# Moving part of a state sum from GpSimd and VectorE to ScalarE and accumulating DMAs, in a macaron block with a selective scan

## What is computed

```
x = x + 0.5 * ffn(layernorm(x))
x = x + ssm(layernorm(x))
x = x + 0.5 * ffn(layernorm(x))
```

```
def step(s, inp):
    u_t, d_t, B_t, C_t = inp
    dA = exp(d_t[..., None] * A)
    dBu = d_t[..., None] * B_t[:, None, :] * u_t[..., None]
    s = dA * s + dBu
    y = einsum('bin,bn->bi', s, C_t)
    return (s, y)
```

## Time and profile before

| | us |
|---|---|
| median of 3 runs | 2955.68 |
| lowest and highest of them | 2943.15, 2956.81 |
| the profiled execution | 2946.41 |
| its span | 2944.6 |
| PE busy | 2434.3 (83% of the span) |
| DVE busy | 2496.5 (85%) |
| POOL busy | 2260.7 (77%) |
| ACT busy | 1754.9 (60%) |

### The profile page before, as it was taken

The page is one execution under the profiler, slowest core; times in us unless marked ns, Lnnn a source line. Parts: engine busy times, 40 slices in busy tenths (PEclk is TensorE's granted clock), DMA queues, the critical chain, the costliest instruction groups (busy, mean ns, idle before and its releaser), DMA issues. The chain is left out here.

```text
span 2944.6 us, 38165 instructions
## 1 busy us (share of the span) xinstructions
PE 2434.3 (83%) x12266; PEld 1988.3 (68%) x12266; DVE 2496.5 (85%) x3131; ACT 1754.9 (60%) x2995; POOL 2260.7 (77%) x1370
## 2 busy tenths in 40 slices
PE   6677778788877898879978899888988796589968
PEld 5566667567666776667756787667776685478757
DVE  5549898788998998899977898899987898899973
ACT  5446567576656666655755557576666566565532
POOL 2238868887986889869996689978798688979852
PEclk9768989888989999989988799898998897699979
DMA  7634562673578367855687356874567555756634
GB/s 272 234 121 146 180 238 98 211 246 130 193 257 297 115 202 242 315 192 161 198 281 270 124 176 215 289 287 135 177 234 284 205 188 206 253 180 203 214 133 141
DMA packets 293951, 606.65 MB, mean 206 GB/s; under 512 B 23024, under 2 KB 23792, under 8 KB 293744
## 3 DMA queue, kind: packets, MB, share of 16 engines
q1 hardware_dynamic: 293744, 604.13, 59.8%
HBM read 451.47 MB, written 152.57 MB: 205 GB/s over the span
## 5 line engine op out<-in xcount | busy, mean ns | idle before, releaser
L1886 POOL TENSOR_TENSOR sbuf<-dus,bring 128x1024 f32<-128x1024 f32 x512 | 1221.9, 2402 | 252.0 <-PE pt L1363 134.1
L1513 ACT ACTIVATE pa<-dls,cst 128x512 f32<-128x512 f32 x1024 | 691.0, 688 | 456.9 <-DVE sbuf L1687 438.1
L1363 PE MATMUL pt<-ident,sbuf 128*128 128x128 f32 x4096 | 663.0, 300 | 244.7 <-DVE sbuf L1687 114.7
L1363 PEld LDWEIGHTS pt<-ident,sbuf 128*128 128x128 f32 x4096 | 527.9, 154 | 389.1 <-DVE sbuf L1687 155.6
L1283 PE MATMUL pm<-xT,wring 128*128 128x512 f32 x2816 | 711.7, 401 | 18.3 <-ACT spx L1427 8.8
L1687 DVE TENSOR_TENSOR_SCAN sbuf<-pa,carry,sbuf 128x512 f32<-128x512 f32 x512 | 635.3, 1267 | 67.5 <-POOL sbuf L1886 44.7
L1687 DVE TENSOR_TENSOR_SCAN sbuf<-pa,sbuf 128x512 f32<-128x512 f32 x512 | 608.7, 1210 | 64.7 <-ACT pa L1513 60.4
L1295 PE MATMUL pm<-wring,act 128*128 128x512 f32 x2176 | 585.9, 413 | 50.8 <-DVE hd L1615 22.6
L1283 PEld LDWEIGHTS pm<-xT,wring 128*128 128x128 f32 x2816 | 518.7, 190 | 121.8 <-issue 20.6
L1698 DVE SCALAR_TENSOR_TENSOR acc<-pt,cT,acc 128x512 f32<-128x512 f32 x768 | 547.6, 737 | 61.3 <-PE pt L1363 57.7
L1295 PEld LDWEIGHTS pm<-wring,act 128*128 128x128 f32 x2176 | 406.2, 195 | 143.9 <-issue 27.3
(11 more groups left out here) (137 smaller groups left out, 2274.6 us busy)
## 6 DMA issues: line engine op xcount, KB each, us to landing
wring<-wsp SPq DMA_DIRECT2D x408, 512.0 KB, 4.3
bring<-b_d SPq DMA_DIRECT2D x256, 256.0 KB, 3.8
xn_d<-tb SPq DMA_DIRECT2D x24, 1024.0 KB, 9.7
xnb<-xn_d SPq DMA_DIRECT2D x19, 1024.0 KB, 7.3
x_d<-tb SPq DMA_DIRECT2D x16, 1024.0 KB, 5.8
u_d<-hd SPq DMA_DIRECT2D x64, 256.0 KB, 4.1
sg_d<-hd SPq DMA_DIRECT2D x64, 256.0 KB, 3.9
tb<-x_d SPq DMA_DIRECT2D x16, 1024.0 KB, 7.3
```

The lines of the kernel that those rows point to most:

```text
L1363: ins = e.matmul(pt[u.pt[tt]][:, k * P:(k + 1) * P], sbuf[:, u.s3, k, tt * P:(tt + 1) * P], ident[:, :], is_transpose=True, start=True, st ...
L1513: e.activation(pa[k % 2][:, :], dls[:, k, :], ACT.Exp, scale=col(C_A + (4 * u.ig + k) * N + u.n)).then_inc(S.a_exp, 1)
L1886: e.tensor_tensor(sbuf[:, u.s3, h * m:(h + 1) * m, :], dus[:, h * m:(h + 1) * m, :], bring[:, u.s2:u.s2 + 1, :].broadcast_to([P, m, TC]), ...
```

## The change

The 15 groups before the last one sum their states in another way. The last group stays as it was.

- States 0, 3, 5, 8, 10 and 13 (`MOVED`): ACT scales all four quarters into `tmp`, which now has four tiles, [128, 4, 512]. No add follows on an engine. The whole tmp goes to y_d by one DMA: for state 0 a plain store, issued by SP; for the other five an accumulating DMA issued by POOL, which adds tmp to what lies in y_d.
- The ten other states are summed in acc by DVE. The first of them, n = 1, writes acc by a multiply alone; it takes the place of ACT's write.
- After state 15 acc is added to y_d by an accumulating DMA issued by POOL; the plain store from SP is gone.
- Each of these seven DMAs waits until the one before it has landed (the semaphores st_t, ac_t, ac_y), and the next moved state can be written to tmp when the DMA from tmp has landed. State 1 of the next group writes acc when the DMA from acc has landed.
- y_d is laid out by partition, so that each row of a DMA is 2048 contiguous elements of 4 bytes. The load of y (L2104 before) is of the same size.
- The planner counts a DMA on POOL with `ISSUE_POOL` = 1.0, and the order of all engines is planned anew. The kernel reserves 8192 as its `dynamic_dma_scratch_size`.

For one group the instructions change as follows:

| | before | after |
|---|---|---|
| ACT, scaled quarters | 16 | 24 |
| DVE, multiply and add | 48 | 36 |
| DVE, multiply alone | 0 | 4 |
| POOL, adds | 12 | 0 |
| POOL, accumulating DMAs of 1 MiB | 0 | 6 |
| SP, plain stores of 1 MiB | 1 | 1 |

```diff
-SHARED = (4, 8, 12)
+SHARED = (0, 4, 8, 12)
+MOVED = (0, 3, 5, 8, 10, 13)
...
             u.last = (c, u.ig) == (NCH - 1, 1)
+            u.moved = not u.last and u.n in MOVED
+            u.shared = u.last and u.n in SHARED
+            u.first = not u.last and u.n == 1
...
+            if u.moved:
+                u.y_before = sf("y_d")
+                u.t_kept = self.up(S.ac_t if u.n else S.st_t, 16)
+                self.sfree["tmp"] = self.sfree["y_d"] = (u.t_kept,)
...
-                u.y_kept = self.y_ready[c, u.ig] = self.up(S.st_y[u.ig], 16)
-                self.add("y_out", u)
+                u.y_before = sf("y_d")
+                u.y_kept = self.y_ready[c, u.ig] = self.up(S.ac_y[u.ig], 16)
...
-        tmp = sb("tmp", [P, TC])
+        tmp = sb("tmp", [P, 4, TC])
...
         def dve_states(units):
-                    if u.n == 0 or u.n in SHARED:
+                    if u.moved or u.shared:
...
+                        if u.first:
+                            e.tensor_scalar(a, x, scale, None, ALU.mult).then_inc(S.v_cmac, 1)
+                        else:
+                            e.scalar_tensor_tensor(a, x, scale, a, ALU.mult, ALU.add).then_inc(S.v_cmac, 1)
...
         def pool_states(units):
-                    if u.n not in SHARED:
-                        continue
-                    for tt in range(4):
-                        q.wait_ge(u.mul[tt], *u.acc_before[tt])
-                        e.tensor_tensor(acc[:, tt, :], acc[:, tt, :], tmp[:, :], ALU.add).then_inc(S.g_cadd, 1)
+                    if u.moved and u.n:
+                        q.wait_ge(u.mul[3], *u.y_before)
+                        e.dma_start(y_d[u.c, u.ig], tmp_row, accum_op=ALU.add).then_inc(S.ac_t, 16)
...
+                    elif u.n == N - 1 and not u.last:
+                        q.wait_ge(u.sum[3], *u.y_before)
+                        e.dma_start(y_d[u.c, u.ig], acc_row, accum_op=ALU.add).then_inc(S.ac_y[u.ig], 16)
...
-        def sp_y_out(units):
-                    q.wait_ge(u.sum[3])
-                    e.dma_start(rows(y_d[:, u.ig * 512:(u.ig + 1) * 512], u.c), acc[:, :, :]).then_inc(S.st_y[u.ig], 16)
+        def sp_t_out(units):
+                    q.wait_ge(u.mul[3], *u.y_before)
+                    e.dma_start(y_d[u.c, u.ig], tmp_row).then_inc(S.st_t, 16)
```

More of the change, by code:

```diff
@@ L65 @@
 DWELL = 12.0
-ISSUE, LAND = 0.42, 2.5
+ISSUE, ISSUE_POOL, LAND = 0.42, 1.0, 2.5
 LATE = {"pe": 0.3, "act": 0.13, "dve": 0.13, "pool": 0.15}
@@ L108, in begin @@
     def begin(self):
-        self.events, self.time, self.up, self.table = [], 0.0, None, None
+        self.events, self.time, self.up, self.table, self.moves = [], 0.0, None, None, False
     def wait_ge(self, *events):
@@ L168, in dma_start @@
         self.time += size / 370e3
+        self.moves = True
         return self
@@ L1229, in macaron @@
         y_rows = xT[:, :, :, :].bitcast(F32)
+        tmp_row = tmp[:, :, :].rearrange("p t n -> p (t n)")
+        acc_row = acc[:, :, :].rearrange("p t n -> p (t n)")
         small_m = NI * XW // 2
```

69 lines of the change are left out of this document (43 added, 26 removed).

## The result

| | us |
|---|---|
| before, median of 4 runs (lowest to highest) | 2950.48 (2943.15 to 2956.81) |
| after, median of 4 runs (lowest to highest) | 3004.65 (2998.87 to 3020.5) |
| ratio after / before, 95% interval | 1.0196 (1.0167 to 1.0224) |
| forecast, range | 2905, 2848 to 3015 |

The changed kernel is 2% slower. The forecast was 1.5% faster; the time lies in the range, and the direction was wrong.

A forecast was written before the change was run, and what follows sets the result against it. The prediction took DVE, POOL and PE to bound the kernel in turns, by stretches of 100 us. From 2946.4 us it took 77 of relief, added 30 for DMA overflow and 5 for landings: 2904, forecast as 2905, range 2848 to 3015.

The follow-up runs named there:

- e3: The changed kernel with y_d laid out by token, so accumulations go in rows of 2 KB instead of 8, same order; 3013.1 us, ratio 1.0232 to before.
- e1: The changed kernel, same order and issues, each of the 90 accumulations cut to 256 of 2048 columns (128 KB); 2878.6 us, ratio 0.9754 to before.

## What to carry to other kernels

Price a new DMA by what it does to the loads around it: how long it holds all engines in one piece, against how far ahead of their use the loads really land. A free mean share says nothing of that. An experiment that shrinks a transfer and leaves all instructions and their order in place parts relief from traffic in one run, and a second one with the same bytes in shorter pieces tells length from amount. And look for the free part of a change first: here more tiles of tmp gave 19 us in one plan, with no traffic at all, and nothing in another.

## What the runs showed of the hardware

- The queue on which GpSimd hands over its DMAs took most of the 16 engines while it had packets: 92.0% against 10.0% for the hardware queue over 6 us of one accumulation, 97.2% against 1.2% in one pair of plain stores, 80 against 21% at the median of after's 90 accumulations.
- Where both queues had rows, these began one for one: 96 and 96 with rows of 8 and 2 KB (after), 478 and 482 with rows of 2 KB on both (e3).
- A transfer of SP that found its own queue empty began 0.96 us after its issue where GpSimd's queue was idle, and 2.4 us after it inside an accumulation of 1 MB (medians).
- An accumulation of 1 MB took 5.57 us of all 16 engines in rows of 8 KB and 6.1 in rows of 2 KB; a plain store from the same queue 2.7.
- The issue of an accumulation is recorded with 0.87 us on GpSimd at the median, one of a plain store with 0.60. The next instruction began after 0.61 and 0.62 us. The records of instructions behind an accumulation's issue are some 0.27 us longer and overlap.
- Some of SyncE's issues took longer, and the median didn't move. One line of weight loads, in ns at least, median, at most; the same line of before had 1405 at most, and in e1 1152. Whether full queues hold it wasn't tried:

```profile
L2007 SPq DMA_DIRECT2D wring<-wsp x168: 319/320/4398, 336.3 to 2906.9; - x168
```
